# The key and value projection with high and low weight halves in one stationary of 128 columns

## The reference, cut to what matters

```python
qkv = jnp.einsum('bsd,ed->bse', x, Wqkv_w) + Wqkv_b
q = qkv[..., :D_MODEL]                                  # 512 columns
k = qkv[..., D_MODEL:D_MODEL + HEAD_DIM]                # 32 columns, for all heads
v = qkv[..., D_MODEL + HEAD_DIM:]                       # 32 columns, for all heads
scores = jnp.einsum('bqhd,bkd->bhqk', q, k) * scale     # causal mask, softmax
ctx = jnp.einsum('bhqk,bkd->bqhd', attn, v).reshape(B, S, D_MODEL)
x = _layernorm(x + ctx @ out_w.T + out_b)
x = _layernorm(x + _L0_ffn_ref(x, router_w, w1, w2, w3))  # 8 experts, the best 2 per token
```

## Time and profile before

| | us |
|---|---|
| median of 3 runs | 1166.06 |
| lowest and highest | 1165.67, 1166.78 |
| the profiled execution, its own time | 1163.79 |
| its span, first to last instruction | 1162.0 |
| TensorE matmuls, busy | 1093.5 |
| VectorE, busy | 890.2 |
| ScalarE, busy | 715.7 |
| mean granted clock of TensorE, share of full | 0.977 |

### The profile page before, as it was taken

How to read it: one execution, slowest core, us unless ns; L and a number is a source line. 1 busy time by engine, 2 the same in 40 slices (tenths; PEclk the granted TensorE clock), 3 DMA queues, 4 the chain that set the end, 5 groups by cost and what they waited for, 6 DMA issues and landing times.

```text
span 1162.0 us, 18342 instructions
## 1 busy us (share of the span) xinstructions
PE 1093.5 (94%) x6056; PEld 523.6 (45%) x6080; DVE 890.2 (77%) x1103; ACT 715.7 (62%) x844; POOL 165.2 (14%) x156
## 2 busy tenths in 40 slices
PE   6699999999999999999989998999999999999976
PEld 4246433743336543333743743374333564333442
DVE  3276778669887689889676668876988868988956
ACT  5444567447884477887436446843788547788821
POOL 2340122011002012001004012020200101200000
PEclk9699999999999999999999999999999999999988
DMA  4992430154001522000164254016400142200000
GB/s 138 222 164 62 122 73 2 53 130 110 1 1 38 128 91 37 1 1 2 50 144 102 57 126 110 1 37 146 109 1 1 38 106 78 37 1 1 2 2 36
DMA packets 41102, 74.37 MB, mean 64 GB/s; under 512 B 14224, under 2 KB 15248, under 8 KB 40976
## 3 DMA queue, kind: packets, MB, share of 16 engines
q1 hardware_dynamic: 25392, 58.74, 19.4%
q0 software_dynamic: 13584, 11.54, 6.6%
q10 hardware_dynamic: 2000, 2.51, 0.8%
HBM read 25.58 MB, written 8.39 MB: 29 GB/s over the span
## 4 chain that ended last, share of the span: by engine, by line
PE 75%; DVE 14%; issue 4%; POOL 2%; SPq 2%; ACT 1%; ACTq 0%; DVEq 0%; DMA 0%; POOLq 0%
PE sc L1087 19%; PE bank L1109 17%; PE sc L974 10%; PE sc L1227 9%; DVE psum_k L773 8%; PE bank L974 7%; PE sc L1127 3%; PE sc L1242 2%; DVE stats L849 2%; PE bank L1127 2%; DVE res L846 2%; SPq L375 2%; POOL prob L474 2%; PE sc L1175 1%; PE bank L1235 1%
## 5 line engine op out<-in xcount | busy, mean ns | idle before, releaser
L602 ACT ACTIVATE prob<-sc 128x1024 f32<-128x1024 f32 x544 | 524.9, 1026 | 167.0 <-PE sc L1087 153.0
L773 DVE TENSOR_TENSOR psum_k<-psum_k,prob 128x2048 f32<-128x2048 f32 x170 | 395.6, 2327 | 5.1
L1087 PE MATMUL sc<-q_st,k_st 128*128 128x512 f32 x1088 | 334.3, 428 | 25.1 <-DMA q_st<-q_lo 8.1
L1087 PEld LDWEIGHTS sc<-q_st,k_st 128*128 128x128 f32 x1088 | 186.8, 191 | 273.7 <-ACT prob L602 180.0
L1109 PE MATMUL bank<-prob,v_sb 128*32 128x512 f32 x2176 | 289.3, 608 | 0.1
L474 POOL TENSOR_SCALAR_AFFINE_SELECT prob<-prob 128x1024 f32<-128x1024 f32 x64 | 86.7, 1391 | 575.2 <-ACT prob L602 575.2
L1227 PE MATMUL sc<-prob,w_sb 128*128 128x512 bf16 x488 | 117.4, 380 | 2.3 <-issue 1.4
L773 DVE TENSOR_TENSOR psum_k<-prob 128x2048 f32<-128x2048 f32 x28 | 64.1, 2289 | 51.9 <-ACT prob L602 46.7
L1109 PEld LDWEIGHTS bank<-prob,v_sb 128*32 128x32 f32 x2176 | 43.9, 108 | 105.9 <-issue 90.0
L632 ACT ACTIVATE prob<-sc 128x512 f32<-128x512 f32 x64 | 38.0, 593 | 75.5 <-PE sc L1227 75.5
L974 PE MATMUL bank<-q_st,wq_hi 128*128 128x512 f32 x240 | 80.8, 401 | 0.0
(11 more groups left out here) (138 smaller groups left out, 997.8 us busy)
## 6 DMA issues: line engine op xcount, KB each, us to landing
q_st<-q_hi SPq DMA_DIRECT2D x128, 128.0 KB, 2.4
q_st<-q_lo SPq DMA_DIRECT2D x128, 128.0 KB, 2.4
res<-in_x SPq DMA_DIRECT2D x8, 1024.0 KB, 5.2
res<-ob_sb POOLq DMA_DIRECT2D x8, 1024.0 KB, 8.1
out_x<-res SPq DMA_DIRECT2D x32, 256.0 KB, 2.5
res<-in_xT SPq DMA_DIRECT2D x7, 1024.0 KB, 5.0
w_sb<-in_w POOLq DMA_DIRECT2D x8, 256.0 KB, 8.7
prob<-in_wqkvT ACTq DMA_DIRECT2D x4, 288.0 KB, 6.1
```

Source lines behind the costliest of these rows:

```text
L602: nc.scalar.activation(prob[t % NP][:, half * HW:(half + 1) * HW], score_half(q // TB, 2 * t + half).rearrange("p m n -> p (m n)"), ACT.Ex ...
L773: nc.vector.tensor_tensor(acc[:, :], first[:, :], prob[t % NP][:, :], ALU.add).then_inc(add_v, 1)
L1087: last = nc.tensor.matmul(dst, k_st[:, k * P:(k + 1) * P], q_st[slot][:, c * HJ:(c + 1) * HJ, at:at + P], start=True, stop=not shift)
```

## The change

`wq_hi` is widened by 64 columns, which hold the low weights of v and k, right of their high ones; `wq_lo` keeps only the q columns. One matmul with a stationary of 128 columns then gives high weights by high x in partitions 0 to 63 of the bank and low weights by high x in 64 to 127. High weights by low x stays a matmul of 64 columns on partitions 0 to 63. The two row halves are added in three steps: ScalarE adds the bias to the lower half and writes `kv_sum` (64 partitions, SBUF), VectorE adds the upper half of the bank to it (`add_kv`), and ScalarE copies k to `k_st` from there. `split_low_k` takes k from `kv_sum` instead of the bank and stands behind the last residual; `add_kv` has its old place. `turn_v` waits for the sum.

```diff
-                last = product(LOW[4][0:2 * HD, :], (wq_hi, wq_lo), (xT_hi, xT_lo), c, slice(D, D + 2 * HD))
+                last = product_kv(c)
...
+            def product_kv(c):
+                def high():
+                    return nc.tensor.matmul(LOW[4], wq_hi[:, c, D:D + 4 * HD], xT_hi[:, c, :],
+                                            start=(c == 0), stop=(c == DC - 1))
+                if c == 0:
+                    high()
+                last = nc.tensor.matmul(LOW[4][0:2 * HD, :], wq_hi[:, c, D:D + 2 * HD], xT_lo[:, c, :],
+                                        start=False, stop=False, skip_group_check=True)
+                return high() if c else last
```

ScalarE and VectorE behind it:

```diff
                 act.wait_ge(projected, count(b, projected, 5 * g + 1))
+                nc.scalar.activation(kv_sum, LOW[4][0:2 * HD, :], ACT.Identity, bias=bvk_sb[:, :]).then_inc(kv_half, 1)
+                act.wait_ge(kv_ready, count(b, kv_ready, g + 1))
-                nc.scalar.activation(vT_sb[:, :], LOW[4][0:HD, :], ACT.Identity, bias=bvk_sb[0:HD, :])
                 for part in (0, 2):
-                    last = nc.scalar.activation(k_st[part * HD:(part + 1) * HD, cols], LOW[4][HD:2 * HD, :],
-                                                ACT.Identity, bias=bvk_sb[HD:2 * HD, :])
+                    last = nc.scalar.activation(k_st[part * HD:(part + 1) * HD, cols], kT_sb, ACT.Copy)
...
+            def add_kv(b, g):
+                dve.wait_ge(kv_half, count(b, kv_half, g + 1))
+                dve.sem_inc(waited_apart, 1)
+                nc.vector.tensor_tensor(kv_sum, LOW[4][2 * HD:4 * HD, :], kv_sum, ALU.add).then_inc(kv_ready, 1)
...
                 for part in (1, 3):
-                    last = nc.vector.scalar_tensor_tensor(
-                        out=k_st[part * HD:(part + 1) * HD, cols], in0=LOW[4][HD:2 * HD, :],
-                        scalar=bvk_sb[HD:2 * HD, :], in1=k_st[0:HD, cols].bitcast(F32),
-                        op0=ALU.add, op1=ALU.subtract)
+                    last = nc.vector.tensor_tensor(k_st[part * HD:(part + 1) * HD, cols], kT_sb,
+                                                   k_st[0:HD, cols].bitcast(F32), ALU.subtract)
...
                         if t == 3:
                             with if_more(dve, b, g):
-                                split_low_k(b, g + 1)
+                                add_kv(b, g + 1)
...
                     with if_more(dve, b, g):
+                        split_low_k(b, g + 1)
                         split_low_q(b, g + 1, 0)
                     normalise(g, 2 * g + 1, x1_ready)
```

In the prologue VectorE cuts the weights of each chunk in two instructions instead of one:

```diff
-                nc.vector.tensor_tensor(wq_lo[:, c, :], wq_raw[c], wq_hi[:, c, :].bitcast(F32),
+                nc.vector.tensor_tensor(wq_hi[:, c, D + 2 * HD:D + 4 * HD], wq_raw[c][:, D:D + 2 * HD],
+                                        wq_hi[:, c, D:D + 2 * HD].bitcast(F32), ALU.subtract)
+                nc.vector.tensor_tensor(wq_lo[:, c, :], wq_raw[c][:, 0:D], wq_hi[:, c, 0:D].bitcast(F32),
                                         ALU.subtract).then_inc(first_low, 1)
```

More of the change, by code:

```diff
@@ L119, in sem @@
             return ctx.enter_context(nc.semaphore(name))
-        wq_hi = sb("wq_hi", [P, DC, D + 2 * HD], F32R)
-        wq_lo = sb("wq_lo", [P, DC, D + 2 * HD], F32R)
+        wq_hi = sb("wq_hi", [P, DC, D + 4 * HD], F32R)
+        wq_lo = sb("wq_lo", [P, DC, D], F32R)
         ow_hi = sb("ow_hi", [P, DC, D], F32R)
@@ L235, in build @@
         low_out = sem("low_out")
+        kv_half = sem("kv_half")
+        kv_ready = sem("kv_ready")
         vT_turned = sem("vT_turned")
@@ L298, in build @@
             stored[0]: 16 * TB * NG // 2, stored[1]: 16 * TB * NG // 2,
[L299 removed]
+            projected: 5 * NG, high_out: 5 * NG, low_out: 5 * NG, kv_half: NG, kv_ready: NG, vT_turned: NG, v_ready: NG,
             scored: 2 * NT, exped: 2 * NT, masked: 2 * NQ, pv_done: NT, add_v: ADDS,
@@ L533, in _ @@
                 act.wait_ge(first_in[c], 2 * 16)
-                nc.scalar.activation(wq_hi[:, c, :], wq_raw[c], ACT.Copy).then_inc(first_high, 1)
+                nc.scalar.activation(wq_hi[:, c, 0:D + 2 * HD], wq_raw[c], ACT.Copy).then_inc(first_high, 1)
                 nc.scalar.activation(xT_hi[:, c, :], xT_raw[0][:, c, :], ACT.Copy).then_inc(first_high, 1)
@@ L734, in judge @@
                                         ALU.mult).then_inc(verdict_ready, 1)
+            add_kv(0, 0)
             split_low_k(0, 0)
@@ L996, in turn_v @@
             def turn_v(b, g):
-                pe.wait_ge(high_out, count(b, high_out, 5 * g + 1))
+                pe.wait_ge(kv_ready, count(b, kv_ready, g + 1))
                 pe.sem_inc(waited_apart, 1)
@@ L1000, in turn_v @@
                     last = nc.tensor.transpose(LOW[5][:, t * HD:(t + 1) * HD],
-                                               vT_sb[:, t * P:(t + 1) * P], ident[0:HD, 0:HD])
+                                               kv_sum[0:HD, t * P:(t + 1) * P], ident[0:HD, 0:HD])
                 last.then_inc(vT_turned, 1)
@@ L1027, in _ @@
                 pe.wait_ge(first_low, 2 * (c + 1))
-                for bank, cols in ((LOW[4][0:2 * HD, :], slice(D, D + 2 * HD)), (q_bank(0, 0), slice(0, P))):
-                    last = product(bank, (wq_hi, wq_lo), (xT_hi, xT_lo), c, cols)
-                    if c == DC - 1:
-                        last.then_inc(projected, 1)
+                last = product_kv(c)
+                if c == DC - 1:
+                    last.then_inc(projected, 1)
+                last = product(q_bank(0, 0), (wq_hi, wq_lo), (xT_hi, xT_lo), c, slice(0, P))
+            last.then_inc(projected, 1)
             for j in range(1, HJ):
```

5 lines of the change are left out of this document (3 added, 2 removed).

## The result

| | before | changed |
|---|---|---|
| median, us | 1166.01 (1165.67 to 1166.78, 4 runs) | 1155.22 (1154.18 to 1157.99, 4 runs) |
| ratio to before | | 0.991, interval 0.9892 to 0.9928 |
| profiled execution: own time, span, us | 1163.79, 1162.0 | 1155.08, 1153.3 |
| mean granted clock of it | 0.977 | 0.981 |

The kernel became 0.9% faster.

A forecast was written before the change was run, and what follows sets the result against it. TensorE's instruction stream was taken as the bound, busy throughout each boundary stretch. Savings of 6.3 us (loop) and 0.8 (prologue) sum to 7.1; profiled 1163.79 becomes 1156.7, plus 2.3 for the median gives 1159.0 us, range 1156.5 to 1162.0.

The forecast's parts named there:

- The matmuls: Key/value projection at seven block boundaries: 8 matmuls instead of 12, about 0.90 us saved at each, 6.3 us.
- The prologue: First projection, ahead of the loop: four matmuls less give 0.92 us, later TensorE start costs 0.13; net 0.8 saved.
- ScalarE and VectorE at a boundary: Moved evictions, addition and low parts of k at each block boundary: later handovers stay hidden and cost nothing.
- cover: Slack at a boundary: TensorE reaches projection q(2) 1.0 us after q_lo(0) is out, hiding the moved work.
- The shared interface: VectorE's low-k subtractions with both inputs in SBUF, beside GpSimd: taken as 0, upper bound 0.6 us lost over seven.
- 1 (saved matmuls stood in a wait): At boundaries, matmuls stood in a wait for the last context tile's low part; only 0.8 won, 1165.3 us; 6%.
- 2 (charge by weight loads): TensorE projections are priced by weight loads, 1.61 to 1.29 us each; 2.6 saved over eight, 1163.5 us; 4%.
- 3: ScalarE and VectorE chain at boundaries: q(2) waits 0.3 to 0.7 us at each, 1161 to 1164 us; 5%.
- 4: Slower: at boundaries TensorE waits for q_lo(0) behind add_kv; 1171.6 us if 2.8 us later than worked out; 3%.
- rival 5: Short low-clock stretches fall elsewhere: one moves a time by 1.6 us either way; inside the forecast's range, which has 82%.

The follow-up runs named there:

- e3: Kernel before with the product of low weights by high x left out for k and v, 8 matmuls per projection instead of 12; 1154.42 us.
- e4: Kernel before with one idle 64-column matmul more per chunk, 16 per key/value projection; 1171.14 us.
- e6: Changed kernel with six idle matmuls ahead of each of three TensorE waits in each attention stage; 1154.47 us.
- e5: Kernel before with six idle matmuls ahead of each of three TensorE waits in each attention stage; 1163.36 us.
- e1: The changed kernel again, unaltered, beside the kernel before in the same rounds; 1153.32 us.
- e2: Changed kernel with one idle 64-column matmul per chunk into an unused bank, so 12 per key/value projection again; 1163.87 us.
- e8: Changed kernel with the idle matmuls of e6, plus twelve idle matmuls ahead of the first real one in the prologue; 1154.58 us.
- e7: Kernel before with the idle matmuls of e5, plus twelve idle matmuls ahead of the first real one in the prologue; 1167.48 us.
- e11: Changed kernel, but VectorE makes the low parts of k right behind the addition, ahead of the last residual; 1156.12 us.
- e12: The changed kernel once more, an unaltered copy, beside the kernel before of the third session; 1154.63 us.
- e9: Changed kernel with four idle matmuls in the prologue's projection alone, so only the loop's seven projections have 8; 1155.72 us.

## Why the prediction was right in direction and too small

**The matmuls (6.3 us for the loop): right.** 8 in 1.83 us at a boundary, 0.93 less than the 2.76 of the earlier trace rows. 32 of them are 7.4 us by spacing, and 6.8, 7.5 and 7.3 by e3, e4 and e6 less e5, but 9.1 by e1 less e2 and 11.7 by e8 less e7: what is shown is the price at the boundaries, by the rows, and not that of the whole program.

**The prologue (0.8): over-sized in its sum, and not settled.** Both instructions of VectorE were as worked out, and the first matmul came at 7.85 (7.91 worked out, wrong from 8.0). But the step "the stream has no hole, so four matmuls less behind 12.04 give 0.92" took the time at which the clock rises as fixed. It rose 1.9 us later in this profile, and over the profiles without idle matmuls ahead of it it lies at 10.7 to 13.9; and at full clock VectorE sets the pace (0.34 in e7 and e8).

**ScalarE and VectorE at a boundary (0): right.** Kept standing for 2.94 us (2.8), the sum out at 212.22 (213.95 worked out, and the whole boundary begins 1.83 us earlier here: 212.12), q(2) without a hole at all seven boundaries, cover 1.2 (1.0). By e2 and e3 the moved work gives or costs no more than one to two microseconds; e11 shows that this cover is real at one boundary, since using it up opens a hole of 0.4.

**The shared interface (0): right in the sum, on the wrong side in its mechanism.** VectorE's subtractions stayed at 683 ns; GpSimd's two instructions together grew from 1.27 to 2.03 us. VectorE waits 0.16 us for them ahead of the normalisation at 216.35, and the first matmul that turns a normalised tile comes at 220.19: nothing of the 0.76 us reaches TensorE. The Trainium skill (VectorE: DVE Perf Modes, Two Vector instructions with no wait between them) has the interface shared and this trace agrees that there is a price, with GpSimd paying it here, where in the earlier trace rows VectorE had 4.88. In both cases the one that started second became the longer one (VectorE at 72.57 behind GpSimd at 72.10; GpSimd at 214.20 behind VectorE at 214.03); no run tests that.

**Rivals.** 1 (saved matmuls stood in a wait) and 2 (charge by weight loads) would leave 0.8 and 2.6 us; e3, e4 and the rows say 7.4. 3 and 4 want a hole ahead of q(2), and there is none at any of the seven boundaries.

**The step that failed is rival 5 and its place in the range:** the low stretches were taken as luck that is the same on both sides ("one more or fewer moves a time by 1.6, in either direction"), priced at no more than 1.6, with no term for TensorE's waits for instructions (the page's chain had "issue" at 4% in both kernels). The range's lower end doesn't follow from its own terms either: 1166.06 less 7.3 and 1.6 is 1157.2, and 1156.5 was written. The measured saving of 10.8 is over the 8.9 of these terms too. What the runs have in its place:

- The changed kernel has the higher clock in all three of its sets: mean 0.9809 over 16 executions (the first set, e1, e12) beside 0.9786 over 57 of before. 0.0024 ± 0.0005 at 0.69 us per 0.001 is 1.6 us. It isn't what fewer matmuls bring as such: e3 has it (0.9823), but e11, the changed kernel with another order on VectorE, doesn't (0.9787).
- A stretch costs 1.5 to 2.0 us in blocks 2 and 6, about half of its 3.3 us, and 0.2 to 0.7 in blocks 3 and 7. So the price of 1.6 was right; that it falls on both sides alike was wrong. Before has five such stretches in blocks 2 and 6 in five profiles, the changed kernel none in three; in blocks 3 and 7 it is eight and three.
- The loop's second pass is 1.1 us shorter (7.84 and 6.70), and the waits for instructions in blocks 4 and 8 by 0.65 and 0.36, from 3 profiles against 5. Timed at equal clock, where these waits stay in, the change is worth 8.2 ± 0.6 and 8.3 ± 0.6, which leaves 0.8 to 0.9 above the 7.4 of the matmuls (and up to 1.8 if the prologue gave nothing).

The 8.2 to 8.3 at equal clock and 1.6 for the clock make 9.8 to 9.9; measured were 10.8, 9.7 and 10.95 (e1 and e12 beside their own before). That the clock's share exists is shown by the clocks, and that the stretches of blocks 2, 3, 6 and 7 hang on waits by e5 to e8; what the shorter waits for instructions are worth is read from profiles and was tested by no run. **Why** the changed kernel escapes the stretch of block 2 behind a wait of the same 2.19 us stays open, and so does what shortens the waits for instructions: a different layout of TensorE's program is an argument and was not tried by itself. No run here beats the changed kernel by more than its scatter.

## What to carry to other kernels

Where TensorE's stream has no hole, take the price of a matmul from the distance between starts, at the clock of that stretch, and multiply: by the rows the seven boundaries gave 6.4 us where 6.3 were worked out. Take the profile of the kernel before several times before calling a low clock stretch or a wait for instructions luck: one that stands in four of five profiles is likely a property of the program, which a change can lose or gain, and it deserves a term and a price of its own. Read that price from the block that it stands in, with and without it. To measure a matmul's worth, add or take matmuls that nobody reads, in more than one version of the kernel, and compare at equal granted clock: the same 32 matmuls came out at 6.8 to 11.7 us here.

## What the runs showed of the hardware that I had not expected

- A low stretch of the clock (0.50 for about 3.3 us) can follow a TensorE wait of 2.0 or 2.19 us: behind the 2.19 us of block 2 it does in four of five profiles of before, behind those of block 6 in one. It costs 1.5 to 2.0 us in these blocks and 0.2 to 0.7 in blocks 3 and 7. Six idle matmuls (1.66 us) in the wait keep the clock at 1.00, and in all such waits raise a kernel's mean clock from 0.9783 to 0.9815.
- With the idle matmuls that bring the clock to its full level earlier in the prologue, whose last q projection starts 1.7 us earlier, the kernel before was 4.1 us slower (e7 beside e5), and the changed kernel as fast as without (e8 beside e6).
- Beside VectorE's subtractions with both inputs in SBUF, GpSimd's two instructions over four elements went from 0.23 and 1.04 us to 0.60 and 1.43, and VectorE's kept to 0.68.
- TensorE waits 1.0 to 3.8 us for instructions as its loop begins its second pass, in one piece or two, and differently for kernels that differ by a few matmuls (e9 2.41, e2 3.05, e5 3.77). Up to about 2.4 us of it cost nothing here, since another wait ends last.
